# The boundary between attention and feed-forward of a fused audio tower: the first group's preparation and its loads placed in the last attention rows, the first two blocks in the drain

## The reference

```python
h = tokenizer(x)                                  # 32 -> 1024 -> 256 per token, silu
h = h + identity_attention(layernorm(h))          # 16 heads, no weights
h = h + ffn(layernorm(h))
# ffn: two layers, on 64 rows x 128 tokens x 256
def _layer(x, ...):
    qkv = shift_token(x) @ wqkv                   # 256 -> 1536, 8 heads of 64
    q, k = l2norm and scales, then rotary
    x = x + local_attention(q, k, v) @ wo         # one window of 128 keys, causal
    h = shift_token(x)
    h = (h - mu) / sqrt(var + 1e-05) * lg + lb
    a, g = split(h @ w1 + b1)                     # 256 -> 2 x 682
    x = x + (a * gelu(g)) @ w2 + b2
```

## Time and profile before

| | us |
|---|---|
| median of 3 runs | 2691.74 |
| lowest, highest | 2688.89, 2692.04 |
| the profiled execution | 2688.39 |
| its span on the core | 2686.6 |
| mean granted clock of TensorE, share of full | 0.989 |
| busy PE, PEld, DVE, ACT, POOL | 2597.5, 2230.8, 1918.4, 1702.8, 1424.5 |

### The profile page before, as it was taken

The page is one execution under the profiler, slowest core; times in us unless marked ns, Lnnn a source line. Parts: engine busy times, 40 slices in busy tenths (PEclk is TensorE's granted clock), DMA queues, the critical chain, the costliest instruction groups (busy, mean ns, idle before and its releaser), DMA issues.

```text
span 2686.6 us, 71253 instructions
## 1 busy us (share of the span) xinstructions
PE 2597.5 (97%) x25088; PEld 2230.8 (83%) x25088; DVE 1918.4 (71%) x3779; ACT 1702.8 (63%) x4184; POOL 1424.5 (53%) x1512
## 2 busy tenths in 40 slices
PE   7999999889999999988999998999999998999998
PEld 5888888768888888877888887888888887888887
DVE  7777777668878788776555646887788777666664
ACT  4666666557777777774444435777777787444442
POOL 7888888477777776652000006777777664000000
PEclk9999999999999999999999999999999999999999
DMA  2111111111111111121111111111111111222221
GB/s 48 37 48 36 44 36 38 40 43 43 51 38 50 41 37 39 41 67 58 58 53 55 52 34 45 40 48 41 50 38 41 40 36 57 69 82 66 80 73 47
DMA packets 165615, 130.35 MB, mean 49 GB/s; under 512 B 23239, under 2 KB 163689, under 8 KB 165462
## 3 DMA queue, kind: packets, MB, share of 16 engines
q1 hardware_dynamic: 163157, 119.80, 14.5%
q0 software_dynamic: 2304, 8.47, 1.1%
HBM read 77.47 MB, written 50.33 MB: 48 GB/s over the span
## 4 chain that ended last, share of the span: by engine, by line
PE 48%; DVE 21%; ACT 20%; issue 7%; SPq 2%; DMA 1%; DVEq 1%; POOL 0%; ACTq 0%; POOLq 0%
ACT attn_E L1058 15%; PE const_banks L1335 6%; PE const_banks L1336 6%; PE const_banks L1337 6%; DVE attn_neg_top L1231 6%; DVE attn_ss L1224 5%; DVE attn_rot_b L1208 5%; ACT attn_sq L1095 5%; PE const_banks L1473 3%; PE const_banks L1472 3%; PE const_banks L1471 3%; PE const_banks L525 3%; PE const_banks L510 3%; PE const_banks L599 2%; PE const_banks L511 2%
## 5 line engine op out<-in xcount | busy, mean ns | idle before, releaser
L1058 ACT ACTIVATE attn_E<-const_banks,attn_nbias,attn_rn 128x128 f32<-128x128 f32 x1024 | 452.8, 461 | 146.2 <-DVE attn_nbias L1236 146.2
L995 POOL TENSOR_TENSOR attn_qk<-attn_rot_a,attn_rot_b 128x1024 f32<-128x1024 f32 x128 | 303.4, 2370 | 354.1 <-issue 288.6
L982 POOL TENSOR_TENSOR ffn_rstd<-ffn_var,const_neg_half 128x4 f32<-128x4 f32 x32 | 32.3, 1009 | 687.9 <-DVE ffn_var L1161 687.9
L1346 PE MATMUL const_banks<-weights_w_hi,attn_xT_hi 128*128 128x512 f32 x768 | 315.3, 411 | 5.4 <-ACT attn_sq L1095 4.3
L1347 PE MATMUL const_banks<-weights_w_lo,attn_xT_hi 128*128 128x512 f32 x768 | 304.3, 396 | 0.0
L1348 PE MATMUL const_banks<-weights_w_hi,attn_xT_lo 128*128 128x512 f32 x768 | 304.0, 396 | 0.0
L1261 DVE SCALAR_TENSOR_TENSOR ffn_gated<-const_banks,weights_b_col,ffn_gate 128x512 f32<-128x512 f32 (+1 forms) x192 | 143.7, 748 | 216.6 <-ACT ffn_gate L1129 209.7
L1335 PE MATMUL const_banks<-ffn_xT_hi,ffn_w_hi 128*128 128x512 f32 x704 | 283.6, 403 | 6.9 <-DVE ffn_xT_lo L1173 5.4
L1336 PE MATMUL const_banks<-ffn_xT_lo,ffn_w_hi 128*128 128x512 f32 x704 | 280.0, 398 | 0.0
L1337 PE MATMUL const_banks<-ffn_xT_hi,ffn_w_lo 128*128 128x512 f32 x704 | 279.3, 397 | 0.0
L1129 ACT ACTIVATE ffn_gate<-const_banks,weights_b_col 128x512 f32<-128x512 f32 x160 | 110.1, 688 | 228.2 <-PE const_banks L1337 222.7
(11 more groups left out here) (179 smaller groups left out, 8009.3 us busy)
## 6 DMA issues: line engine op xcount, KB each, us to landing
attn_x_res<-xa SPq DMA_DIRECT2D x128, 128.0 KB, 4.9
xb<-attn_x_new SPq DMA_DIRECT2D x128, 128.0 KB, 1.7
ffn_x_<-xb SPq DMA_DIRECT2D x32, 512.0 KB
h<-ident_h SPq DMA_DIRECT2D x64, 128.0 KB, 1.7
xa<-ident_n SPq DMA_DIRECT2D x64, 128.0 KB, 1.7
attn_x_<-xa SPq DMA_DIRECT2D x128, 64.0 KB
xa<-ffn_x_new SPq DMA_DIRECT2D x16, 512.0 KB, 3.6
ffn_add<-h SPq DMA_DIRECT2D x16, 512.0 KB, 6.5
```

The lines of the kernel that those rows point to most:

```text
L995: pool.tensor_tensor(qk[:, slot].rearrange("p a n -> p (a n)"), rot_a[:].rearrange("p a h d -> p (a h d)"), rot_b[:].rearrange("p a h d -> ...
L1058: last = act.activation(E[:, r, i], ps_s[:, r, i * P:(i + 1) * P], ACT.Exp, bias=nbias[:, r, i:i + 1], scale=rn[:, slot, h:h + 1], accum_o ...
L1346: pe.matmul(out_, xT_hi[:, slot, k], w.w_hi[:, k, cols], start=(k == 0), stop=False)
```

## The change

- **Loads.** All group loads become four pairs, one pair for each row (`load_group_row`): 127 x 512 B and 128 x 1 KB each. For groups 0 and 1 they stand in steps 54 to 61, one pair a step, between the load of x and the load of x_res. SP's last 12 steps and DVE's last 4 before the drain are written out instead of looped (`tail`).
- **Preparation of group 0.** Statistics and power move from step 65 to step 62, normalise from 66 to 63. The turn moves to step 65, ahead of the q and k transposes, into banks 3 and 4; ACT's gain and bias stand at the head of step 65, ahead of the exponentials, PE waits for them, and group_high and group_low follow later in step 65.
- **Blocks.** Block 0 moves to the end of step 65 and block 1 (into banks 5 and 6, once the last scores are used) to the end of step 67; both stand ahead of the last output projection in step 68. The gelu and product of block 0 are in step 67, the gelu's table is loaded in step 66, in front of the ET copies. The wait for the last x_new moves from block 1 to block 3. In step 66 the weighting of the values (`weigh`) and its copy stand ahead of the transposes of E.

```diff
...
-    for t in range(count, count + depth):
+    for t in range(end, count + depth):
...
+        ps_T_first = banks[:, 3:5]
+        h_first = [banks[:, 5], banks[:, 6]]
...
                 need(sp, st, 32 * (t + 1))
+            for r in range(GROUP):
+                load_group_row(sp, layer, t, u, r)
+
+        def load_group_row(sp, layer, t, u, r):
             local = t - layer * GROUPS
-            sp.dma_start(y[1:P, u, :, 0:P], shifted(xb, local)).then_inc(y_ld[u], 16)
-            sp.dma_start(y[:, u, :, P:3 * P], rows(xb, local)).then_inc(y_ld[u], 16)
+            sp.dma_start(y[1:P, u, r, 0:P], shifted(xb, local)[:, r]).then_inc(y_ld[u], 16)
+            sp.dma_start(y[:, u, r, P:3 * P], rows(xb, local)[:, r]).then_inc(y_ld[u], 16)
...
-                if step == ROWS and layer == 0:
+                if step == ROWS - 10 and layer == 0:
                     sp.wait_ge(y_pad, 1)
-                if step in (ROWS, ROWS + 1):
-                    load_group(sp, layer, layer * GROUPS + step - ROWS, layer * GROUPS // 4, step - ROWS)
+                if step is not None and ROWS - 10 <= step < ROWS - 10 + 2 * GROUP:
+                    g, r = divmod(step - ROWS + 10, GROUP)
...
+                    load_group_row(sp, layer, layer * GROUPS + g, g, r)
...
-            run_from(sp, L, ROWS, 6, body, before)
+            run_from(sp, L, ROWS, 6, body, before, tail=12)
...
-                if step == ROWS + 1:
+                if step == ROWS - 2:
...
-        def group_high(act, layer, t, u):
+        def group_gains(act, layer, t):
+            src = ps_T if not isinstance(t, int) or t % GROUPS else ps_T_first
...
-                if step == ROWS + 3:
-                    group_high(act, layer, layer * GROUPS, 0)
+                if step == ROWS + 1:
+                    group_gains(act, layer, layer * GROUPS)
...
+                if step == ROWS + 1:
+                    group_high(act, layer, layer * GROUPS, 0)
...
+                if step == ROWS + 2:
+                    o_high(act, t - 4)
+                    act.activation(ask[:], c["neg_half"][:, 0:1], ACT.Gelu)
...
-                if on(4):
-                    b = t - 4
...
-                if step == ROWS + 4:
-                    act.activation(ask[:], c["neg_half"][:, 0:1], ACT.Gelu)
+                if step == ROWS + 3:
+                    gate_of(act, layer, layer * GROUPS + 1, 1, 0)
+                if on(4) and step != ROWS + 2:
+                    o_high(act, t - 4)
...
-                    group_statistics(dve, layer * GROUPS, layer * GROUPS // 4, 0)
+                    group_low(dve, layer * GROUPS, 0)
...
-                if step == ROWS + 2:
-                    group_normalise(dve, layer * GROUPS, 0)
+                if step == ROWS + 3:
+                    block_of(dve, layer, layer * GROUPS + 1, 1, 0)
...
-                if step == ROWS + 3:
-                    group_low(dve, layer * GROUPS, 0)
-
-            run_from(dve, L, ROWS, 5, body, before)
+                if step == ROWS - 2:
+                    group_statistics(dve, layer * GROUPS, layer * GROUPS // 4, 0)
+                if step == ROWS - 1:
+                    group_normalise(dve, layer * GROUPS, 0)
+
+            run_from(dve, L, ROWS, 5, body, before, tail=4)
...
-            if p == 1 and isinstance(t, int) and t == layer * GROUPS + 1:
-                pe.wait_ge(s["x_done"], (layer + 1) * ROWS)
+            if isinstance(t, int) and t == layer * GROUPS + 1:
+                if p == 1:
+                    pe.wait_ge(s["exp_done"], 2 * ROWS * (layer + 1))
+                if p == 3:
+                    pe.wait_ge(s["x_done"], (layer + 1) * ROWS)
...
-                if step == ROWS + 4:
-                    pe.wait_ge(w.f_split, w.STRIPS * (layer + 1))
-                    hidden(pe, layer, layer * GROUPS + 1, 1, 0)
+                if step == ROWS + 1:
+                    pe.wait_ge(s["et_done"], 2 * (t - 3))
+                    group_turn(pe, layer * GROUPS)
+                    pe.wait_ge(f["xg"], KD * (layer * GROUPS + 1))
...
+                if step == ROWS + 2:
+                    weigh(t, u)
...
+                if on(4) and step != ROWS + 2:
+                    weigh(t, u)
...
-                if step == ROWS + 2:
-                    need(pe, s["exp_done"], 2 * (L + ROWS))
-                    group_turn(pe, layer * GROUPS)
+                if step == ROWS + 1:
+                    pe.wait_ge(w.f_split, w.STRIPS * (layer + 1))
+                    pe.wait_ge(s["squared"], L + ROWS)
+                    hidden(pe, layer, layer * GROUPS + 1, 1, 0)
+                if step == ROWS + 3:
+                    hidden(pe, layer, layer * GROUPS + 1, 1, 1)
...
-                    if on(1) and not (step == 1 and p == 0):
+                    if on(1) and not (step == 1 and p < 2):
...
```

More of the change, by code:

```diff
@@ L614, with run_from @@
 G_AT = 64
-def run_from(eng, base, count, depth, body, before=None, loop=True):
+def run_from(eng, base, count, depth, body, before=None, loop=True, tail=0):
     head = -(-(depth + 2) // 4) * 4 if loop else count
+    end = count - tail if loop else count
     def peeled(t):
@@ L633, in run_from @@
     if loop:
[L634 removed]
+        with eng.Fori(head // 4, end // 4) as i:
             for u in range(4):
                 body(4 * i + (base + u), i + base // 4, u, lambda lag: True)
[L637 removed]
+    for t in range(end, count + depth):
         peeled(t)
@@ L1040, in group_high @@
                 need(act, f["xT_lo"], KD * (t - 1) + kk + 1)
-                act.activation(yg[:, kk], ps_T[:, kk], ACT.Identity, bias=b_col[:, layer, kk:kk + 1],
+                act.activation(yg[:, kk], src[:, kk], ACT.Identity, bias=b_col[:, layer, kk:kk + 1],
                                scale=g_col[:, layer, kk:kk + 1]).then_inc(f["xg"], 1)
+        def group_high(act, layer, t, u):
             for kk in range(KD):
@@ L1046, in group_high, with o_high, gate_of @@
                 act.activation(yT_hi[:, u % 2, kk], yg[:, kk], ACT.Copy).then_inc(f["xT_hi"], 1)
+        def o_high(act, b):
+            need(act, s["o_ps"], b + 1)
+            need(act, s["out_ps"], b)
+            act.activation(oT_hi[:].rearrange("p k n -> p (k n)"), ps_v[:], ACT.Copy).then_inc(s["oT_hi"], 1)
+        def gate_of(act, layer, t, u, p):
+            k, j = ORDER[p], KH * (t - 1) + p
+            need(act, f["h_ps"], j + 1)
+            need(act, f["gated_done"], j - 1)
+            bias, src = b1_col[:, layer], h_banks(layer, t, p)
+            if k < FULL:
+                act.activation(gate[:, p % 2], src[1], ACT.Gelu, bias=bias[:, FULL + k:FULL + k + 1]
+                               ).then_inc(f["gate_done"], 1)
+            else:
+                g_rows = slice(G_AT, G_AT + HTAIL)
+                act.activation(gate[0:HTAIL, p % 2], src[0][g_rows], ACT.Gelu, bias=bias[g_rows, TAIL:NB]
+                               ).then_inc(f["gate_done"], 1)
         def attention_scalar(act, layer, before=None):
@@ L1123, in body @@
                         j = KH * (t - 1) + p
[L1125 to L1134 removed]
+                        if not (step == 1 and p == 0):
+                            gate_of(act, layer, t, u, p)
                         need(act, f["gated_done"], j + 1)
@@ L1296, in body @@
                     if on(1):
-                        block_of(t, u, p)
+                        if not (step == 1 and p == 0):
+                            block_of(dve, layer, t, u, p)
                         if p:
@@ L1349, in project, with weigh @@
                 return last
+            def weigh(t, u):
+                b = t - 4
+                need(pe, s["et_done"], 2 * b + 2)
+                need(pe, s["v_done"], min_int(t, L + ROWS))
+                need(pe, s["oT_lo"], b)
+                for j in range(HEADS // 2):
+                    for r in range(2):
+                        h = 2 * j + r
+                        last = pe.matmul(ps_v[r * HD:(r + 1) * HD, j * P:(j + 1) * P],
+                                         v[:, u, h * HD:(h + 1) * HD], ET[:, r, j], start=True, stop=True)
+                last.then_inc(s["o_ps"], 1)
             def body(t, i, u, on):
```

55 lines of the change are left out of this document (19 added, 36 removed).

## The result

| | before | after |
|---|---|---|
| median us (6 runs each) | 2691.2 | 2669.57 |
| lowest, highest | 2688.89, 2692.04 | 2667.61, 2674.05 |
| span of the profiled execution | 2686.6 | 2665.8 |
| mean granted clock | 0.989 | 0.993 |

The changed kernel takes 0.9924 of the time before, 95% interval 0.9914 to 0.9934: 21.6 us by the medians, 20.8 between the two profiled spans. The forecast was 2676.7, 15 us less than before. The profiled execution of the change, at 2667.61, is the fastest of its six.

The account below looks back on a forecast made before the run. PE bounds the rows; at the boundaries its idle time and low clock delay group 1's turn. Per boundary 9.1 - 1.0 - 0.7 = 7.4 us, two 14.8, say 15: 2691.74 - 15 = 2676.7 us, range 2667 to 2689.

Parts of the forecast that it names:

- rival (a): Whole kernel: the forecast itself, 2676.7 us, own range 2670 to 2682; chance 0.70.
- chain behind the last exponential: Drain, last exponential of row 63 to the end of the last output projection: 17.9 us shrinks to 8.9, gaining 9.0.
- last exponential, but for the clock: Exponentials of row 63: net 0.5 us late a boundary, bounds 0 and 2.0.
- clock: New drain: low-clock stretches on PE cost 1.0 us a boundary, bounds 0 and 2.8.
- x_res: Eight rows before step 62: extra loads make x_res late, costing 0.7 us a boundary, bounds 0 and 3.1.
- product of block 0 ahead of the statistics: Behind x_new of row 63: block 0's product (0.7 us) no longer stands before group 1's statistics.
- from the statistics to the turn: Group 1: nothing changes in this stretch, which travels whole; DVE's four normalises last 4.54 us at the first boundary.
- 2.0 us late: DVE, steps 62 and 63: 3.4 us of added statistics and normalise delay it by 2.0, range 0 to 3.4.
- rival (d): Loads on one DMA engine: x_new 2.4 us late each row, 18 us a boundary, 2712 in all; chance 0.08.
- The wait of PE before block 3: Behind x_new of row 63: PE waits about 1.8 us, turn not late for it at the first boundary.
- rival (b): Drain: DVE's lateness, low clock and x_res give most back, leaving 1.7 us a boundary, 2688; chance 0.12.
- Rival (c): Another wait pins group 0's turn, block 0 ends behind the exponentials; 4 us more a boundary, 2685; chance 0.10.

Follow-up runs that it names:

- experiment 5: The changed kernel with ACT's table load for the gelu moved behind the two ET copies of row 63; 2668.40 us.
- experiment 2: The kernel before with only DVE's last four attention steps written out, nothing moved; 2689.07 us.
- experiment 4: The changed kernel with two rows of a group loaded in each of steps 54 to 57, not one in each of eight steps; 2670.76 us.
- experiment 6: The changed kernel with group 1's statistics, power and normalise done early, in steps 66 and 67; 2664.84 us.

## Why the prediction was right, and where it was not

The forecast of rival (a) held in direction, in place and in its main mechanism, the shorter chain behind the last exponential; it was 6.6 us short by the medians, 5.8 by the two traces. By its own terms, in us a boundary (plus is time gained):

| term | forecast | 1st boundary | 2nd boundary |
|---|---|---|---|
| chain behind the last exponential | 9.0 | 8.8 | 7.6 |
| last exponential, but for the clock | -0.5 | 0.7 | 0.7 |
| clock | -1.0 | -0.9 | 0 |
| x_res | -0.7 | 0 | 0 |
| product of block 0 ahead of the statistics | 0.6 | 0.65 | 0.65 |
| from the statistics to the turn | 0 | 0.7 | 1.4 |
| sum | 7.4 | 9.9 | 10.4 |

- **"The chain shrinks by 17.9 - 8.9 = 9.0 us":** 17.9 to 9.2 at the first boundary. The sum was right, its members were not all: the table load (1.5) is not in it (experiment 5), the division and the transposes of E and the projection of row 62 are. That is partly luck: the ET copies behind the table load end at 1207.25 and PE comes to the weighting at 1207.36, so the path that was forecast and the one that counted are equally long. At the second boundary the old chain was 16.7, with less low clock in it (0.83 in 2270 to 2280 where 1200 to 1210 had 0.66), and gives 7.6.
- **"2.0 us late", "net 0.5":** x_new of row 59 is 0.8 us later than before at both boundaries. Against experiment 2, which has the written-out steps and no statistics in them, it is 1.7 later: the insertion costs about what I took, and 0.95 comes back from DVE's `tail`, which I had counted for SP alone. So the last exponential is 0.7 sooner at the second boundary and, with the low stretch of the clock, 0.2 later at the first. x_new of row 63 is 8.6 and 8.25 sooner; forecast 8.5, hit with a term too low and others too high.
- **x_res, -0.7 a boundary, and rival (d):** wrong. I paired an issue with the wrong use; the slack is 13.2 us, not 3.1. Twice the stream costs nothing (experiment 4). With that slack neither term nor rival could come about: 0.7 too much taken off, twice. The 0.2 us a row that written-out issues were to give back no run shows, and nothing hung on them.
- **The clock, -1.0 a boundary:** of the right size where it fell, 0.9 us at the first boundary between x_new of rows 60 and 61; at the second the clock did not fall. That it does not fall each time I had as a bound only. DVE's `tail` (0.95), unforeseen, made up for it.
- **"From the statistics to the turn nothing changes":** 9.64 to 8.97 at the first boundary, where POOL's split still pins it (it ends at 1221.35, the turn starts at 1222.21). At the second, 7.1 to 5.6: no split runs there, PE arrives at the turn behind its own blocks, one fewer than before (2.9 us), but for its new wait of 1.7. I had treated both boundaries alike.

The wait of PE before block 3, forecast as 1.8 to 2, is 1.7 at both. Of rival (b) there is the 1.7 us of the insertion and the 0.9 of the clock at one boundary, on top of which the x_res bound did not come. Rival (c) has nothing for it: the turn of group 0 waits 0.4 us, and the q and k transposes wait for POOL, not for the gain.

What the parts are worth by themselves: the loads alone 3.4 (0.5 to 5.9), the tail alone 1.8 (not clear of zero), the blocks 6.5 taken from the change. If they added up, some 10 of the 21.6 us would be left for the early preparation with the reordered step 66; that remainder was not run apart, and neither was the early weighting alone.

## What to carry to other kernels

Before you price a transfer's slack, count its buffers and find which use it is issued for; the nearest consumer in the timeline may be the one before it. A wait that two boundaries share should be worked out at each, if one of them lacks the neighbour that sets it. Where the same program passes a place twice, compare the two passages first: their difference, 0.9 us of clock here, is what a single trace cannot tell from an edit. And an engine without gaps is not thereby the bound: what said so were two written-out rows of 9.8 us beside looped ones of 10.05, and the loops of three engines held 26 us (14.7 + 11.7).

## What was unexpected of the hardware

- A loop on an engine costs time on the chain of a pipelined row: 0.15 to 0.17 us a row for DVE, 5.1 us (ScalarE) and 7.0 us (TensorE) for two layers of 64 rows, though DVE and ScalarE wait for others in each row and TensorE is busy for all of it.
- While POOL's cast (1216.36 to 1217.84) and elementwise split (1217.91 to 1221.35) ran, four normalises of DVE took 5.72 us instead of 1.38. The first ended 0.14 us behind the cast, the second 0.15 us behind the split, and the other two took 0.4 us each:

```profile
1217.90 3.60 DVE L1198 TENSOR_SCALAR ffn_xn<-ffn_x_,ffn_mv,ffn_rstd 128x256 f32<-128x256 f32 x1
```

  The Trainium skill (SBUF — State Buffer, section SBUF: two separate sides) says that GpSimd and a DVE instruction in a two-port mode share one pair of ports as an exclusive lock for a whole instruction. The trace agrees, though it does not say in which mode the normalise ran, and in experiment 6, where the normalise ran before the split, it took 1.38 us again.
- One load of 127 partitions, split in rows, still moves 21 GB/s at a DMA share of 0.07 in experiment 4, as in the earlier trace rows; twice as many ahead of x_res made no engine but SP wait.
